# Cross-attention's softmax: the maximum subtracted by GpSimd for four heads at once, and one exponential of 512 elements in place of four with a bias

## The reference

```
x = layernorm(x + self_attention(x))                 # 16 heads of 64, causal
x = layernorm(x + cross_attention(x, ctx, mask))     # 16 heads of 8, key mask
x = layernorm(x + experts(x))                        # 8 experts, top 2, width 256

# cross-attention, per sequence
scores = (q @ k.T) / sqrt(8)
scores = where(mask == 0, -1e9, scores)
attn   = softmax(scores)                             # exp(s - max) / sum
out    = (attn @ v) @ Wo.T + bo
```

## Time and profile before

| What | Value |
|---|---|
| median of 3 runs | 268.04 us (267.89 to 268.69) |
| the profiled execution | 267.57 us, its span 265.8 us |
| PE busy | 241.4 us, 91% |
| DVE busy | 188.3 us, 71% |
| ACT busy | 167.5 us, 63% |
| POOL busy | 98.6 us, 37% |
| share of PE in the chain that ended last | 76% |
| mean granted TensorE clock | 0.973 |

### The profile page before, as it was taken

The page is one execution under the profiler, slowest core; times in us unless marked ns, Lnnn a source line. Parts: engine busy times, 40 slices in busy tenths (PEclk is TensorE's granted clock), DMA queues, the critical chain, the costliest instruction groups (busy, mean ns, idle before and its releaser), DMA issues.

```text
span 265.8 us, 6740 instructions
## 1 busy us (share of the span) xinstructions
PE 241.4 (91%) x2222; PEld 209.0 (79%) x2222; DVE 188.3 (71%) x928; ACT 167.5 (63%) x556; POOL 98.6 (37%) x154
## 2 busy tenths in 40 slices
PE   0798969999999999999989998967998999999992
PEld 0787858788788888787866876846798999999992
DVE  1475626959869869869879699575367885586885
ACT  2468566988988988988888977535744733333000
POOL 3386994536436446737626333130003000010111
PEclk9999997999999999999999999995799999999999
DMA  6997000000000000000000000000000000000000
GB/s 213 370 350 295 1 4 0 4 0 4 1 2 1 2 2 2 2 0 2 1 1 2 4 0 4 0 4 0 0 2 0 2 1 2 1 22 0 21 22 20
DMA packets 6435, 9.09 MB, mean 34 GB/s; under 512 B 1025, under 2 KB 4737, under 8 KB 6017
## 3 DMA queue, kind: packets, MB, share of 16 engines
q1 hardware_dynamic: 4032, 7.09, 7.4%
q10 hardware_dynamic: 2368, 1.57, 2.2%
HBM read 8.14 MB, written 0.52 MB: 33 GB/s over the span
## 4 chain that ended last, share of the span: by engine, by line
PE 76%; DVE 7%; POOL 5%; ACT 5%; issue 3%; DMA 2%; POOLq 0%; SPq 0%; DVEq 0%; ACTq 0%
PE bank L1194 10%; PE bank L885 9%; PE bank L887 8%; PE bank L886 8%; PE bank L1033 6%; PE bank L976 5%; PE bank L1002 5%; PE bank L1049 5%; PE bank L1105 5%; PE bank L1018 4%; PE bank L1064 4%; ACT probs_s L441 2%; DMA raw<-in_wqT 2%; POOL mask_add L408 1%; POOL probs_s L311 1%
## 5 line engine op out<-in xcount | busy, mean ns | idle before, releaser
L441 ACT ACTIVATE probs_s<-masked_s,nmax_s 128x128 f32<-128x128 f32 x128 | 49.8, 393 | 7.4 <-PE bank L1018 3.7
L311 POOL TENSOR_TENSOR probs_s<-probs_s,rec_sum_s 128x512 f32<-128x512 f32 x32 | 33.3, 1041 | 54.2 <-DVE rec_sum_s L615 54.1
L444 ACT ACTIVATE probs_c<-masked_c,nmax_c 128x128 f32<-128x128 f32 x128 | 40.3, 393 | 6.7 <-DVE nmax_c L607 6.7
L885 PE MATMUL bank<-ctx_hi,gu_hi 128*128 128x256 f32 x128 | 39.9, 312 | 0.0
L482 ACT ACTIVATE silu<-bank 128x256 f32<-128x256 f32 x54 | 20.5, 385 | 30.5 <-PE bank L887 30.5
L886 PE MATMUL bank<-ctx_lo,gu_hi 128*128 128x256 f32 x128 | 36.6, 286 | 0.0
L887 PE MATMUL bank<-ctx_hi,gu_lo 128*128 128x256 f32 x128 | 36.5, 285 | 0.0
L607 DVE CUSTOM_DVE_ANT_0 masked_s<-bank,causal 128x128 f32<-128x128 f32 x128 | 29.4, 286 | 4.7 <-PE bank L976 4.4
L607 DVE CUSTOM_DVE_ANT_0 masked_c<-bank,mask_add 128x128 f32<-128x128 f32 x128 | 29.0, 285 | 0.1
L885 PE MATMUL bank<-x_hi,w_hi 128*128 128x256 f32 x64 | 21.6, 338 | 8.2 <-DVE w_lo L581 8.2
L885 PEld LDWEIGHTS bank<-ctx_hi,gu_hi 128*128 128x128 f32 x128 | 25.2, 197 | 1.5 <-issue 1.4
(11 more groups left out here) (156 smaller groups left out, 596.6 us busy)
## 6 DMA issues: line engine op xcount, KB each, us to landing
raw<-in_gateT SPq DMA_DIRECT2D x1, 1024.0 KB, 5.3
raw<-in_upT SPq DMA_DIRECT2D x1, 1024.0 KB, 7.4
down_sb<-in_down SPq DMA_DIRECT2D x1, 1024.0 KB, 9.4
raw<-in_wkT ACTq DMA_DIRECT2D x2, 256.0 KB, 4.7
raw<-in_wqT SPq DMA_DIRECT2D x2, 256.0 KB, 5.1
raw<-in_wvT SPq DMA_DIRECT2D x1, 512.0 KB, 6.2
ctxT_all<-in_ctxT SPq DMA_DIRECT2D x1, 512.0 KB, 7.5
wo_sb<-in_woT SPq DMA_DIRECT2D x1, 512.0 KB, 5.6
```

Source lines behind the costliest of these rows:

```text
L311: pool.tensor_tensor(probs_s[:, g % 2], probs_s[:, g % 2], spread(rec_sum_s[:, 4 * g:4 * g + 4], 2, S), ALU.mult).then_inc(normed, 1)
L441: last = act.activation(probs_s[:, g % 2, i, :], masked_s[:, g % 2, i, :], ACT.Exp, scale=-1.0, bias=nmax_s[:, h:h + 1], accum_out=rsum_s[ ...
L444: last = act.activation(probs_c[:, g % 2, i, :], masked_c[:, g % 2, i, :], ACT.Exp, scale=-1.0, bias=nmax_c[:, h:h + 1])
L885: pe.matmul(dst, wh, xh, start=True, stop=False)
```

## The change

For cross-attention a new step is put between DVE's maxima and ACT's exponential. `shift_c` on GpSimd subtracts the four heads' `nmax_c`, each spread over its 128 keys, from `masked_c` in place, in one instruction of 128 x 512 elements. ACT then takes exp(-masked_c) of all 512 elements in one instruction with no bias, and waits for the new semaphore `shifted` in place of `maxed["c"]`. Self-attention is as it was. In GpSimd's list `shift_c` of groups 2 and 3 of sequence n-2 stands behind `split_gu` and `own_k`, ahead of `normalise(0, n)`; that of groups 0 and 1 of sequence n-1 stands behind `normalise(3, n)`, ahead of the second `root`, `padded_v` and `split_x2`.

```diff
+            def shift_c(g, n):
+
+                if on(n):
+                    pool.wait_ge(maxed["c"], NG * n + g + 1)
+                    pool.tensor_tensor(masked_c[:, g % 2], masked_c[:, g % 2], spread(nmax_c[:, 4 * g:4 * g + 4], 2, S),
+                                       ALU.subtract).then_inc(shifted, 1)
@@ -395,6 +402,8 @@
                     split_gu(piece)
                 if n > 0:
                     own_k(n)
+                shift_c(2, n - 2)
+                shift_c(3, n - 2)
                 normalise(0, n)
                 root(var1_done, pow1_done, mv1, n - 1)
                 add_out_bias(n - 2)
@@ -409,6 +418,8 @@
                     split_x(2)
                     split_x(3)
                     own_k(0)
+                shift_c(0, n - 1)
+                shift_c(1, n - 1)
                 root(var2_done, pow2_done, mv2, n - 2)
                 padded_v(n - 1)
                 split_x2(n - 3)
@@ -433,16 +444,17 @@
             def exp(kind, g, n):
                 if not on(n):
                     return
+                wait(act, turned[kind], NG * n + g - 1)
+                if kind == "c":
+                    act.wait_ge(shifted, NG * n + g + 1)
+                    act.activation(probs_c[:, g % 2].rearrange("p h t -> p (h t)"),
+                                   masked_c[:, g % 2].rearrange("p h t -> p (h t)"), ACT.Exp, scale=-1.0).then_inc(exped[kind], 1)
+                    return
                 act.wait_ge(maxed[kind], NG * n + g + 1)
-                wait(act, turned[kind], NG * n + g - 1)
                 for i in range(4):
                     h = 4 * g + i
-                    if kind == "s":
-                        last = act.activation(probs_s[:, g % 2, i, :], masked_s[:, g % 2, i, :], ACT.Exp, scale=-1.0,
-                                              bias=nmax_s[:, h:h + 1], accum_out=rsum_s[:, h:h + 1])
-                    else:
-                        last = act.activation(probs_c[:, g % 2, i, :], masked_c[:, g % 2, i, :], ACT.Exp, scale=-1.0,
-                                              bias=nmax_c[:, h:h + 1])
+                    last = act.activation(probs_s[:, g % 2, i, :], masked_s[:, g % 2, i, :], ACT.Exp, scale=-1.0,
+                                          bias=nmax_s[:, h:h + 1], accum_out=rsum_s[:, h:h + 1])
                 last.then_inc(exped[kind], 1)
```

More of the change, by code:

```diff
@@ L217, in build_decoder @@
         mixed = {k: sem(f"mixed_{k}") for k in "sc"}
-        (rec_s, normed, cat_first, cat_last, wo_s, res1_done, stat1_done, aggr1_done, var1_done, pow1_done, x1_ready, x1bo_done,
+        (rec_s, shifted, normed, cat_first, cat_last, wo_s, res1_done, stat1_done, aggr1_done, var1_done, pow1_done, x1_ready, x1bo_done,
          x1T_ps, x1T_evac, cq_proj, cq_evac) = [sem(n) for n in (
-             "rec_s normed cat_first cat_last wo_s res1_done stat1_done aggr1_done var1_done pow1_done x1_ready x1bo_done "
+             "rec_s shifted normed cat_first cat_last wo_s res1_done stat1_done aggr1_done var1_done pow1_done x1_ready x1bo_done "
              "x1T_ps x1T_evac cq_proj cq_evac").split()]
```

## The result

| | median | runs |
|---|---|---|
| before | 267.97 us | 267.66 to 268.69 (4) |
| after | 275.69 us | 272.81 to 276.16 (4) |
| ratio | 1.0262 | 95% interval 1.0189 to 1.0335 |

The change makes the kernel 7.7 us slower; 274.2 us was forecast, in a range of 271.2 to 277.0. The profiled execution took 275.73 us with a span of 273.9. The four times of the changed kernel lie 3.4 us apart, those of before 1.0, and that turns out to be part of the answer.

A forecast was written before the change was run, and what follows sets the result against it. PE alone was taken to pace the steady part. Two waits 3.8, iteration 8 0.8 and one clock fall 1.6 summed to 6.2 us on 268.04, forecasting 274.2 us, range 271.2 to 277.0.

The forecast's parts named there:

- PE sets the pace of the steady part: Steady iterations: PE is busy for all of its 19.14 us, so work taken off ACT gives nothing by itself.
- Rival (d): Steady iterations: ACT is the real pace, so the kernel is no slower or faster, 261 us at most gain; chance 0.05.
- The prices, 0.62 and 1.04 us: Each cross-attention group: one exponential of 512 elements on ACT takes 0.62 us, the new subtraction on POOL 1.04.
- Two waits of 1.9 us, in POOL's order: POOL's iterations 5 and 6, with two split_gu pieces: PE waits 1.9 us each for a copy behind exp c2; +3.8 us.
- Iterations with one piece lose nothing: Iterations 1 to 4, one split_gu piece each: no loss; the tightest, 4, has 0.1 us to spare, 0 to 0.3 possible.
- Iteration 8, +0.8 us: Iteration 8, PE without other work: longer chain for c0 and c1 adds 0.8 us, bounds 0.4 and 2.0.
- the late `root`: Iteration 8: second root ends near 183.2, DVE 2 us late, but PE is covered; without cover up to 1.2 us more.
- The clock, one fall of 1.6 us taken for two waits: Behind the two new PE waits: one fall from 2.4 to 1.2 GHz, +1.6 us, bounds 0 and 3.1.
- Rival (c), contention: POOL takes the port from DVE in layernorm passes: 0 to 0.7 us more, in iteration 8; chance 0.07.
- Rival (a): The clock falls at neither of the two new waits: 272.6 us; chance 0.20.
- Rival (e): The change does nothing: shorter stalls, ACT's relief meets the added latency; within 0.8 us; chance 0.05.

The follow-up runs named there:

- e5: The changed kernel without the subtraction: one exponential of the plain scores, 512 elements at once, behind DVE's maxima; 264.34 us, ratio 0.9872.
- e1: The changed kernel with POOL's split_gu pieces from iteration 2 on moved behind add_out_bias and normalise(1), where POOL idles; 269.41 us, 1.0055 of before.
- e3: The changed kernel, but only groups c0 and c1 of each sequence are subtracted on POOL, the others going the old way; 270.12 us, ratio 1.0078.
- e4: The changed kernel, but only groups c2 and c3 of each sequence are subtracted on POOL, the others going the old way; 267.85 us, ratio 0.9997.
- e9: The changed kernel with split_gu's pieces spread so that only iteration 5 has two, iterations 6 and 7 one each; 272.5 us, ratio 1.0164.
- e11: e1's order, but only the last sequence's four groups are subtracted on POOL, the other seven sequences going the old way; 269.81 us, ratio 1.0058.
- e10: The changed kernel run again unaltered, for its spread and a second profile; 275.94 us, ratio 1.0244, the profiled execution 273.39 us.
- e7: e2 with own_k(1) and iteration 1's piece of split_gu also moved behind add_out_bias; 265.86 us, ratio 0.9913 to before.
- e2: The kernel before the change, with the same move of split_gu as in e1 (iterations 2 on); 267.86 us, 0.9985 of before.

## Why the prediction was right, point by point

- **PE sets the pace of the steady part.** Shown, by e5 above all: 2.5 us of ACT less per iteration, no change in the iteration. Rival (d) is out.
- **The prices, 0.62 and 1.04 us.** 0.631 and 1.040.
- **Two waits of 1.9 us, in POOL's order.** The trace has them at the place named, L1076 waiting for the copy, 1.79 and 1.78 us, and the offsets grow by 2.00 and 1.98 with what surrounds them. e1, e3, e4 and e9 show the cause: not the subtraction, not its place alone, but both halves' passes together in the iterations with two pieces.
- **Iterations with one piece lose nothing.** 0.10 in iteration 3 of PE, the tight one (iteration 4 of POOL); but 0.25 us in iteration 2 by another way, contention (below). The slack is small: in e9, with one piece in iteration 7, PE waits 0.71 us there.
- **Iteration 8, +0.8 us.** 1.05 in the trace, 1.4 to 1.8 in those of e1, e3 and e11, about 1.5 by their medians. The step was mis-sized: the added latency was taken as 0.4 for c0 and 0.4 more for c1; it measured 0.52 and 0.53, and the longer low clock that follows in some executions (0.5 to 0.7 us) was not in the sum. That the late `root` would be covered was right.
- **The clock, one fall of 1.6 us taken for two waits.** One fall in the profile, none in e10's, 1.58 us at the fall. The change less e1 is 6.3 us; less the 4.0 of waits and the 0.35 of small ones, which e1 doesn't have either, about 1.9 are left for the clock, a little more than one fall. So taking one was a fair middle, and a single execution can have none: seven of ten runs had the lower clock. The price of one fall was worked out from the low stretch near 40 us as 1.55 us. There it doesn't hold: without this stretch e1 gains 0.9 us and e7, which then waits for POOL, nothing. That it held behind the first new wait, where PE had nothing else to wait for, is in part luck. Waits (0.2), small ones (0.35), the clock and iteration 8 share the 1.5 us by which the forecast was low. The Trainium skill's rule on longer gaps ("TensorE: Matmul & The Clock Gate", "HAM oscillation"), weighed in the prediction, would have left this term out; waits of 1.8 us were enough in the profiled execution.
- **Rival (c), contention.** Real, 0.25 us, but in a steady iteration and not in iteration 8 as I had put it. The mistake was to reckon with DVE's free time: PE was waiting for this very pass. The Trainium skill ("GPSIMD Engine Reference", section 8) names contention with DVE instructions in a two-port mode or with two SBUF inputs; whether this pass is one of them no run shows, only that it ended just after the POOL instruction that it met.
- **Rival (a)**, no fall, is what e10's profile shows: 273.39 us, against 272.6 forecast for it. As the median it is out. **Rival (e)** is out by the result.

## What to carry to other kernels

Before moving work to an engine that is half idle, write down its list in time for the tightest iteration: POOL was idle for 63% of the span, and that did not help in the two stretches where two subtractions, two pieces of `split_gu` and `own_k` stood ahead of the pass that was wanted. Look for whoever is queued behind the new waiter on the next engine; PE stood still for a copy that the change never touched. Work with a late deadline, like `split_gu`, belongs behind work with an early one, and finding such pieces paid (e7, 2.0 us less than e2) where the change cost.

## What the runs showed of the hardware that was not expected

- Waits of under 2 us can cost almost their own length again by the clock (1.58 us behind one of 1.79), and not every time: the same program, with the same two waits of 1.8 us, ran with no fall of the clock behind them in 273.39 us and with one in 275.73. Of the five such waits in three profiles (after, e10, e9) one was followed by a fall.
- A longer wait is no certain sign either: the wait of 2.6 or 2.7 us that ends at about 40 us was followed by low clock in ten profiles and in e1's, where it was 2.64, by none.
- What a fall costs differs with what follows: 1.58 us behind the first new wait, where PE waited for nothing else; near 40 us 0.9 (e1 against before), or nothing in the end where a wait for POOL follows (e7 against e2).
- A DVE pass of 0.34 us from SBUF to SBUF took 1.33 when it began together with a POOL pass of 1.26 us with two SBUF inputs, and 0.76, three times, when it met the 0.62 us cast L343. In all these it ended less than 0.1 us after the POOL instruction that it met.
